# A fused Mamba, mixture-of-experts and attention block: y of the first chunk partly summed by TensorE, and four smaller moves

## The reference, cut to what matters

```
# x: 2 x 2048 tokens x 256; D_INNER 512, D_STATE 16, 4 experts (top 2)
xn = layernorm(x); x_br, z = split(xn @ W_in)
xb = silu(causal_conv4(x_br) + conv_b)
Bm, Cm = xb @ W_b, xb @ W_c;  delta = softplus(xb @ W_delta + b_delta)
h_t = exp(delta_t * A) * h_(t-1) + delta_t * B_t * xb_t     # per channel and state
y_t = sum over 16 states of h_t * C_t + xb_t * Dp
x = layernorm(x + (y * silu(z)) @ W_out + x)
logits = gelu(x @ rW1 + rb1) @ rW2 + rb2; probs = softmax(logits)
x = layernorm(x + sum over the 2 best experts of probs * (gelu(x @ We1) @ We2 + be2))
x = layernorm(x + attention16heads(x, with an added cross-product term))
x = layernorm(x + relu(x @ W1 + b1) @ W2 + b2)
```

## Time and profile before

| | |
|---|---|
| median of 3 runs | 3641.55 us (3640.53 to 3644.67) |
| the profiled execution, its own time | 3645.86 us |
| its span in the trace | 3644.1 us |
| PE, DVE, ACT, POOL busy | 91%, 78%, 60%, 42% |
| chunk 0 begins its scan | 60.4 us |
| chunks 1 to 7 begin theirs | 234.2, 429.8, 628.0, 828.8, 1028.2, 1226.0, 1423.8 us |
| last scan of chunk 7 ends | 1605.9 us |

### The profile page before, as it was taken

The page is one execution under the profiler, slowest core; times in us unless marked ns, Lnnn a source line. Parts: engine busy times, 40 slices in busy tenths (PEclk is TensorE's granted clock), DMA queues, the critical chain, the costliest instruction groups (busy, mean ns, idle before and its releaser), DMA issues. The chain is left out here.

```text
span 3644.1 us, 41261 instructions
## 1 busy us (share of the span) xinstructions
PE 3312.8 (91%) x14448; PEld 1552.3 (43%) x14448; DVE 2839.1 (78%) x3484; ACT 2176.2 (60%) x3604; POOL 1527.7 (42%) x1294
## 2 busy tenths in 40 slices
PE   4239999999999999989889999999999999998998
PEld 2025556555655555555522222322222222222666
DVE  5898899999989899974468888888888888882444
ACT  5355666656565756532157777777777777777221
POOL 2998899999999999971010000000000000000110
PEclk8679999999999999999999999999999999999999
DMA  3111223131222212232020000000000000000010
GB/s 109 32 38 52 73 70 102 63 112 64 94 84 82 87 62 93 73 121 85 26 97 19 19 19 19 19 17 17 15 17 19 19 19 19 19 10 7 23 35 29
DMA packets 108187, 180.19 MB, mean 49 GB/s; under 512 B 13989, under 2 KB 81689, under 8 KB 99417
## 3 DMA queue, kind: packets, MB, share of 16 engines
q1 hardware_dynamic: 107992, 177.72, 15.5%
HBM read 151.58 MB, written 26.08 MB: 49 GB/s over the span
## 5 line engine op out<-in xcount | busy, mean ns | idle before, releaser
L1927 DVE TENSOR_REDUCE tile_max<-ps 128x1 f32<-128x1024 f32 x976 | 1149.9, 1220 | 248.2 <-PE ps L1723 248.2
L1866 ACT ACTIVATE probs<-ps 128x512 f32<-128x512 f32 x2048 | 1106.4, 598 | 375.4 <-PE ps L1736 373.8
L1486 POOL TENSOR_TENSOR vals<-vals,c_sb 128x512 f32<-128x512 f32 x512 | 681.5, 1363 | 131.9 <-DVE state L1278 111.0
L1273 DVE TENSOR_TENSOR_SCAN vals<-stacks,state,ps 128x512 f32<-128x512 f32 x512 | 655.0, 1279 | 103.0 <-POOL heads_v L1497 38.1
L1736 PE MATMUL ps<-stacks 101*128 101x512 bf16 x2048 | 701.8, 382 | 24.7 <-PEq L245 12.2
L1497 POOL TENSOR_TENSOR heads_v<-heads_v,vals 128x512 f32<-128x512 f32 x512 | 648.0, 1298 | 8.7 <-issue 0.2
L1723 PE MATMUL ps<-stacks 99*128 99x512 bf16 x1952 | 583.8, 380 | 0.0
L227 POOL COPY heads_v<-vals 128x256 f32<-128x256 f32 x32 | 12.7, 402 | 1344.7 <-PE ps L1746 1322.2
L1746 PE MATMUL ps<-probs,heads_v 128*32 128x512 f32 x4096 | 545.3, 605 | 0.0
L731 PE MATMUL ps<-x1T,e_w 128*128 128x512 f32 x1024 | 464.1, 599 | 26.2 <-ACT hid L1041 26.2
L1736 PEld LDWEIGHTS ps<-stacks 101*128 101x128 bf16 x2048 | 195.7, 96 | 658.9 <-ACT probs L1866 423.2
(11 more groups left out here) (201 smaller groups left out, 3055.1 us busy)
## 6 DMA issues: line engine op xcount, KB each, us to landing
e_w<-in_e_w SPq DMA_DIRECT2D x64, 1024.0 KB, 7.1
c_sb<-scratch_c SPq DMA_DIRECT2D x128, 256.0 KB, 3.4
stacks<-scratch_q SPq DMA_DIRECT2D x192, 64.0 KB
stacks<-scratch_k SPq DMA_DIRECT2D x192, 64.0 KB
scratch_q<-parts SPq DMA_DIRECT2D x16, 384.0 KB, 4.2
scratch_k<-parts SPq DMA_DIRECT2D x16, 384.0 KB, 4.4
xr<-scratch_x SPq DMA_DIRECT2D x10, 512.0 KB, 4.4
xn_tok<-in_x SPq DMA_DIRECT2D x8, 512.0 KB, 4.9
```

The costliest lines, as they stand in the source:

```text
L1273: v.tensor_tensor_scan(h[:, n % 2, m, :], decay[:, n % 2, m, :], ps[:, 0, :], state[:, n, m:m + 1], ALU.mult, ALU.add).then_inc(s["h_ready ...
L1486: last = nc.gpsimd.tensor_tensor(h[:, n % 2, m, :], h[:, n % 2, m, :], c_sb[:, n % C_RING, :], ALU.mult)
L1866: fn(probs[:, step % 2, qc, :], ps[:, S_BANK[i], :], ACT.Exp)\
L1927: v.tensor_reduce(tile_max[:, t, half:half + 1], ps[:, at:at + PAIR, :].rearrange("p a n -> p (a n)"), AX.X, ALU.max).then_inc(s["max_read ...
```

## The change

1. First chunk, y: TensorE adds the products of blocks 0 to 2 in PSUM (`sum_y`, an identity matrix as weights, y's start from xb * Dp, then 16 slots); POOL adds block 3 alone. `sum_y(n-1)` stands at the end of PE's slot n, and the scan waits for `y_summed` as well as for `y_added`.
2. First chunk, preparation: convolution, SiLU and projections go by blocks. `project_first` runs delta and B/C with the blocks of xb as outer loop, each as soon as its SiLU is done; ACT takes the absolute value and DVE the relu (`relu_first`) straight from PSUM; both exponentials, then both logarithms share a table load.
3. Router's logits: `logit_parts` computes four partial products, each of 32 weight columns, into four groups of 32 PSUM partitions, with 512 tokens as moving columns; ACT copies them (`copy_logits`), and `fold_logits` adds and transposes them with 4 small matmuls. `project_x` of the next chunk stands around them. DVE's `logits` and `conv(f, 1)` move from the middle of slot 6 to the end of slot 5.
4. Choice of experts: one subtraction and one comparison with a constant array `margin` in place of 6 comparisons.
5. `split_bias`: the first bf16 part and the middle one are written by ACT (`scale_bias`, `cast_bias`), DVE does a subtraction at the end of slot 9 and one at the end of slot 10. SP stores them in its slot 11 in place of 9.
6. DVE's `down(m, 2, 0)` moves from the middle to the end of slot 13, `deltas(f, 0)` from the middle to the end of slot 14, `deltas(f, 1)` from the end of slot 14 to the middle of slot 15.
7. The edge of the convolution: chunks 0 and 4, whose halo counts as zero, skip it, and the multiplication with `keep` is gone.

```diff
+            def sum_y(n):
+                pe.wait_ge(s["hc_ready"], n + 1)
+                if n == 0:
+                    pe.wait_ge(s["y_begun"], DB)
+                    pe.wait_ge(s["abs_ready"], DB)
+                    for m, at in enumerate(FIRST_Y):
+                        mm(ps[:, at, :], ident[:], y[:, m, :], start=True, stop=False)
+                for m, at in enumerate(FIRST_Y):
+                    last = mm(ps[:, at, :], ident[:], h[:, n % 2, m, :], start=False, stop=n == NS - 1)
+                last.then_inc(s["y_summed"], 1)
...
+            def logit_parts(c):
                 wait_free(pe, c, ("logits", 0))
                 wait_read(pe, c, ("router", RB - 1))
-                for i in range(TT):
-                    for k in range(RB):
-                        last = mm(bank(("logits", 0))[:, i * NE:(i + 1) * NE],
-                                  rh[:, k, i * P:(i + 1) * P], r_w2[:, k, :],
-                                  start=k == 0, stop=k == RB - 1)
+                for k in range(RB):
+                    last = mm(bank(("logits", 0))[k * ROWS:(k + 1) * ROWS], r_w2[:, k, :], rh[:, k, :],
+                              start=True, stop=True)
                 full(last, ("logits", 0))
+            def fold_logits(c):
+                wait_free(pe, c, ("logits", 1))
+                wait_read(pe, c, ("logits", 0))
                 for i in range(TT):
+                    last = mm(bank(("logits", 1))[:, i * NE:(i + 1) * NE], lgT[:, i * P:(i + 1) * P], fold[:],
+                              start=True, stop=True)
+                full(last, ("logits", 1))
...
             def scan(c, n, m):
                 if m == 0:
                     at_least(dve, s["y_added"], c * NS + n - 1)
+                    if c * NS + n - 1 <= NS:
+                        at_least(dve, s["y_summed"], c * NS + n - 1)
...
-                for j in range(NE):
-                    for lo, hi, op in ((0, j, ALU.is_gt), (j + 1, NE, ALU.is_ge)):
...
+                v.tensor_tensor(beats[:], prob[:].rearrange("p s j -> p j s").unsqueeze(3).to_broadcast([P, NE, TT, NE]),
+                                prob[:].unsqueeze(1).to_broadcast([P, NE, TT, NE]), ALU.subtract).then_inc(s["margin_ready"], 1)
+                dve.wait_ge(s["margin_ready"], c + 1)
+                v.tensor_tensor(beats[:], beats[:], margin[:], ALU.is_ge).then_inc(steps, 1)
...
-                for m in range(DB):
+                for m in range(DB) if c > 0 else range(len(FIRST_Y), DB):
                     last = nc.gpsimd.tensor_tensor(y[:, m, :], y[:, m, :], h[:, n % 2, m, :], ALU.add)
```

More of the change, by code:

```diff
@@ L355, in mamba_moe_qkv @@
         w2_loaded = [sem("w2_loaded0"), sem("w2_loaded1")]
-        order = [("router", i) for i in range(RB)] + [("logits", 0)]
+        order = [("router", i) for i in range(RB)] + [("logits", 0), ("logits", 1)]
         order += [("up", e, i) for e in range(NE) for i in range(HB)]
@@ L838, in iteration @@
                     quota[0] = START.get((i, n), 0)
+                    if i == 1 and n == 0:
+                        sum_y(NS - 1)
                     if n == 0:
@@ L917, in iteration @@
                         for part in range(2):
-                            if inside(f):
+                            if inside(f) and not first(f):
                                 project_delta(f, 2 * (n - 12) + part)
@@ L930, in iteration @@
                         broadcast(f, 0)
+                    if i == 0 and n > 0:
+                        sum_y(n - 1)
                     while quota[0] > 0:
@@ L1045, in routers, with copy_logits @@
                     gelu(c, ("router", i), rh[:, i, :], col("r_b1", i))
+            def copy_logits(c):
+                wait_full(act, c, ("logits", 0))
+                read(fn(lgT, bank(("logits", 0)), ACT.Copy), ("logits", 0))
             def logit_exps(c):
@@ L1158, in iteration @@
                         norm0(i + 2)
-                    if n == 13 and inside(f):
+                    if n == 13 and inside(f) and not first(f):
                         copy_delta(f, 3)
@@ L1162, in iteration @@
                         norm0(1)
-                    if n == 14 and inside(f):
+                    if n == 14 and inside(f) and not first(f):
                         soft_exp(f, 1)
                         soft_log(f, 1)
+                    if n == 10 and inside(q):
+                        cast_bias(q)
                     if inside(m):
@@ L1177, in iteration @@
                         copy_cw(m)
-                    if n == 11 and inside(f):
+                    if n == 11 and inside(f) and not first(f):
                         copy_bc(f)
@@ L1408, in iteration @@
                         crossed(q)
[L1409 to L1412 removed]
                     if n == 7 and i == chunks:
                         keys(q)
[L1415 to L1416 removed]
                     if inside(m):
[L1418 removed]
+                        for j in range(4):
                             if n == SLOT_OF_DOWN[j] + 1:
@@ L1422, in iteration @@
                             base(m)
+                    if n == 15 and inside(f):
+                        deltas(f, 1)
                     if inside(i):
@@ L1432, in iteration @@
                         norm1_stats(m)
+                    if n == 5 and inside(m):
+                        logits(m)
+                    if n == 5 and inside(f) and not first(f):
+                        conv(f, 1)
                     if n == 0 and inside(q):
@@ L1445, in iteration @@
                         set_stacks(range(1, ROT))
-                    if n == 4 and inside(f):
+                    if n == 4 and first(f):
+                        conv_first()
+                    elif n == 4 and inside(f):
                         conv(f, 0)
                     if n == 9 and inside(q):
-                        split_bias(q)
+                        rest_bias(q)
+                    if n == 10 and inside(q):
+                        last_bias(q)
+                    if n == 12 and first(f):
+                        for blk in range(DB):
+                            relu_first(blk)
                     if n == 12 and inside(f):
                         split_bc(f)
+                    if n == 13 and inside(m):
+                        down(m, 2, 0)
                     if n == 14 and inside(m):
```

230 lines of the change are left out of this document (148 added, 82 removed).

## The result

The changed kernel takes 3601.77 us (median of 4 runs, 3600.94 to 3602.57), the kernel before 3642.2 on the same chip: ratio 0.9888, 95% interval 0.9872 to 0.9904. That is 40 us less; 54 were forecast. The time lies inside the stated range of 3574 to 3613, but 14 us above the forecast of 3588 and at the times of rivals A (3600) and C (3602). The range holds these rivals too, so the time alone doesn't tell which of the mechanisms is right; the stretches and the experiments do. The profiled execution took 3602.57 us with a span of 3600.8, against 3644.1 before: 43.3 less in the span.

What follows compares the result with a forecast made beforehand. In chunks 2 to 6 PE with ACT's answers was taken as the longest cycle, DVE hardly shorter. Terms -7.1 - 8 - 7 - 24 - 4 - 4 = -54 from the median 3641.55 gave 3588 us, range 3574 to 3613.

Steps and rivals of the forecast that it cites:

- Rival A: Chunk 0 gains nothing, as `sum_y` runs at half clock throughout: 0 instead of -8, 3600 us; chance 0.13.
- rival C: Another engine, DVE, holds the middle chunks: 2 us a chunk in place of 4.8, 3602 us; chance 0.13.
- Start: Before the first scan: PE goes on without a pause, first scan at 53.3 in place of 60.37, -7.1 us.
- Chunk 0: First chunk: POOL's waits go, new waits for `sum_y` come; -8 us, bounds -14 to 0.
- Logits on PE: From the router's last matmul to the first `up`: 5.7 us for 9.8, -4.1 a chunk.
- Rival B: Column groups don't overlap, or the switch costs PE 2 us or more: 2.6 less per logits, 3608 us; chance 0.08.
- DVE's operations: Comparisons take 2.4 us for 3.76, -1.3; `split_bias` falls from 6.0 us to two subtractions of 1.65, -2.7.
- The middle chunks: Chunks 2 to 6: about 194 us each, PE gaining 4.2 a chunk; -24 us, bounds -10 to -30.
- All of it, 6 to 7 us, lies behind `keys`: DVE's savings and shorter waits fall in the part of the chunk where PE gains 4.2 us.
- a pair half a slot later costs nothing as long as PE is the later one: Moved `deltas` pairs cost 0, since ACT's decays of the next slot 0 come only behind the last GELU.
- Chunk 1 and chunk 7: Chunk 1 gains by the logits, -7 us (-3 to -9); chunk 7 by shorter POOL waits, -4 (-2 to -6).
- Behind the last scan: Tail, where PE alone sets the pace: the logits and next passes take 5.7 us for 9.9, -4 (-1 to -6).

Runs made afterwards that it cites:

- two blocks: Changed kernel with TensorE summing y of two blocks in chunk 0, not three, and GpSimd adding the other two: 3597.83 us.
- experiment 6: Changed kernel with DVE's six comparisons and the split of the key bias in slot 9 on DVE as before: 3625.38 us.
- experiment 1: Changed kernel with DVE reading `down(m,2,0)` in the middle of slot 13 again, not at its end: 3594.32 us.
- experiment 2: Changed kernel with both pairs of `deltas` back at their old places, middle and end of slot 14: 3597.88 us.
- kernel 3: Changed kernel with both `down(m,2,0)` and the pairs of `deltas` back at their old places: 3588.93 us.
- experiment 9: Changed kernel with `down(m,2,0)` and the pairs of `deltas` at old places, but the pairs late while chunks 0 and 1 are scanned: 3589.84 us.
- experiment 10: Kernel 3 and the kernel of experiment 9, each with y of two blocks summed on PE in chunk 0: 3585.07 and 3584.11 us.

## Why the prediction was right, and where it was off

**Start: right.** Delta and B/C follow the first projections without a pause and end at 41.0, where 41.2 was forecast; the first scan stands at 53.01. First and last row of them on PE, for those of the earlier trace rows:

```profile
23.67 3.60 PE L674 MATMUL ps<-vals,w_delta 128*128 128x512 f32 x8
...
39.98 1.02 PE L678 MATMUL ps<-vals,w_bc 128*96 128x512 f32 x2
```

No experiment took this part of the change back, nor the edge of the convolution; the -7.4 us is read from the two traces.

**Chunk 0: mechanism right, size off.** Forecast -12.4 of POOL's waits, -2 of shorter DVE operations, +6.2 of waits for `sum_y`. Measured: the waits for POOL went; DVE's busy time is only 1.0 lower (152.59 to 151.57), waits for the sums are 7.7, and 0.8 of small other waits are new. The scans of slots 2 and 3 wait 3.50 and 1.24 (forecast 3 and 1.2); plain slots cost 2.9 in three slots, where 2 was forecast for six. With two blocks 5.6 us of these waits go. Nearly all of the 4.7 is the sum's, for without it chunk 0 is back at 173.6. With two blocks it gives 9.1, more than was forecast for three. Rival A (sums at half rate throughout, and no gain) is half true in its rates: the sums that stood behind other work took 2.74 to 2.84 us, and the eight that came after PE had been idle for 2.3 to 6.6 us took 4.35 to 5.49. Its price is not: chunk 0 gave 4.7. The Trainium skill, "TensorE: Matmul & The Clock Gate", What's actually happening, has half rate as the state of an idle engine; these rows agree.

**Logits on PE: right to 0.3 us.** 5.5 for the forecast 5.7, and in the tail 0.87, 1.07, 0.80 and 1.03 us with a next `up` of 1.96 for 3.75. Rival B is out: 1.06 for both groups of four parts. The Trainium skill, "TensorEngine Tiling (Array Packing)", Key Properties, names a drain at each change of mode. In chunk 5 the parts hold PE from 1056.59 to 1057.58, 0.99 us; two passes of 512 columns in a row at the pitch of `up` (12 in 5.31) are 0.9, so for drains 0.1 us is left.

**DVE's operations: right.** 2.45 for the forecast 2.4, and 2.9 for 3.3. The two comparisons take as long as a POOL operation (POOL's took 1.23 to 1.34), as assumed. The Trainium skill, "GPSIMD Engine Reference", section 1. Specifications, names contention with instructions of two SBUF inputs; both have two, and the 1.25 and 1.20 us agree.

**The middle chunks: the step that failed.** "All of it, 6 to 7 us, lies behind `keys`" took DVE's savings as whole, and "a pair half a slot later costs nothing as long as PE is the later one" took the moves at nothing. PE was not the later one. DVE ends these chunks (experiment 6: 20.1 of 23.0 us come through), and each moved piece made a wait that goes round: the late read of `down(m,2,0)` stops PE 1.56 us and then DVE 2.2 us (experiment 1); the late pair holds back the last blocks, POOL, `gated` and PE's `project_out` (experiment 2). DVE's part before `keys` wasn't left as it was either: the additions there end 1.5 us later (83.1 us behind the first scan of chunk 5, and 81.9 in kernel 3), and PE gains 2.8 us at the first `down`, not 4.2. Taking both moves back gives 193.4 a chunk: the forecast of 194 was that of the change without its moves. This is rival C in its effect (another engine holds the chunks, 2 us a chunk in place of 4.8; measured 3.3) and its time, 3602. The prediction named the sign beforehand: it would be wrong "if POOL's waits for DVE stay at 9 us a chunk", and they stayed at 46.0 us in five chunks at L1406 alone, where 46.4 stood before; with both places early they are 32.3. It named a second sign, "if DVE is the one that ends chunks 2 to 6", and experiment 6 shows that too. So the total is right by a range that took rival C in, and for the middle chunks the forecast's mechanism is not what happened.

**Chunk 1 and chunk 7: right** (-7.5 and -3.9): with the old logits chunk 1 gives 6.6 back, and with DVE's old work chunk 7 gives 4.5 back. **Behind the last scan: right in size by chance.** PE's rows at the logits show the forecast 4.2 us, but they don't make the -3.5. With the old logits this stretch takes 2034.6 us, all but the same, and the kernel with two blocks, whose instructions behind chunk 0 are those of the changed kernel, takes 2038.2 there, as long as before. Where the 3.5 comes from stays open. PE had also waited 7.11 us in slot 13 of chunk 7 for the late read:

```profile
1542.06 2.47 PE L798 MATMUL ps<-e_w,hid 128*128 128x256 f32 x5 [7.11 <-DVE x_tok L1487]
```

That wait isn't what eats the gain: in experiment 1 it is 1.8 us, but PE then waits 3.8 for `gated`. From chunk 7's first scan to attention's first exponential the changed kernel takes 423.4 us, with the read early 423.4, with the pairs early 418.5, with both 415.5. With the old logits it is 422.2 with late places and 422.5 with early ones. So there the logits pay, 7 us in these two profiles, only with both places early.

One sum in the forecast doesn't come out: 4.1 + 1.65 makes 5.75 us by which PE would be ahead, not 5.4. Nothing else in it uses the figure.

## What to carry to other kernels

When two engines are nearly level, cost each moved piece against the engine that will be the later one after the change, and look for whoever next writes the PSUM bank that the piece reads. Test such a placement again after each gain: the same places cost 12.8 us with the new logits and nothing, or gave 4.6, with the old. Give an idle engine only as much of a chain's work as takes the other below the bound: two blocks did that, and the third only lengthened the chain.

## What the runs showed of the hardware

Four matmuls of 512 columns behind the same eight 4-column passes took 3.41 us in one kernel and 1.96 in another, with the same instructions around them and the same PE busy time and clock in the 6 us before. A few us won ahead of such a place can be lost in it: a gain of 4.1 us before the tail was no gain (experiment 9), one of 2.3 was kept in the profiles (experiment 10).

DVE's operations of `deltas` took 1.22 us at 128x1024 while GpSimd was idle, and 2.14 and 2.17 while it was in its own operations, here before the first scan and in chunk 2 of the changed kernel:

```profile
51.08 1.22 DVE L1382 TENSOR_TENSOR stacks<-stacks,vals 128x1024 f32<-128x1024 f32 x1
...
587.80 2.17 DVE L1382 TENSOR_TENSOR soft<-vals 128x1024 f32<-128x1024 f32 x1
```

4.6 us more of DVE's busy time a chunk lengthened the chunk by 4.0, although DVE is busy only 91% of the changed kernel's chunks 2 to 6 (893.61 of 977.58) and PE 95%.
